# Scores and row maxima trade their banks: a two-layer attention and expert kernel on one core

## The reference

```
xn = layernorm(x)
s  = attention_part(xn)
g  = silu(expert_part(xn))
x  = x + s * g
```

```
scores = einsum('bhsd,bhtd->bhst', q_embed, k_embed) / D ** 0.5
attn   = softmax(scores, axis=-1)
out    = einsum('bhst,bhtd->bhsd', attn, v) @ wo.T
```

## Time and profile before

| | before |
|---|---|
| median of 3 runs | 1664.55 us (1663.07 to 1669.39) |
| the profiled execution | 1678.29 us, span 1676.5 us |
| PE busy | 1125.7 us (67%) |
| DVE busy | 1108.0 us (66%) |
| ACT busy | 684.1 us (41%) |
| POOL busy | 509.7 us (30%) |
| mean granted TensorE clock | 0.778 |

### The profile page before, as it was taken

How to read it: one execution, slowest core, us unless ns; L and a number is a source line. 1 busy time by engine, 2 the same in 40 slices (tenths; PEclk the granted TensorE clock), 3 DMA queues, 4 the chain that set the end, 5 groups by cost and what they waited for, 6 DMA issues and landing times.

```text
span 1676.5 us, 16891 instructions
## 1 busy us (share of the span) xinstructions
PE 1125.7 (67%) x5366; PEld 589.4 (35%) x5366; DVE 1108.0 (66%) x1815; ACT 684.1 (41%) x1166; POOL 509.7 (30%) x513
## 2 busy tenths in 40 slices
PE   4465667677766722446656177999977878787886
PEld 4332334343433410222212023888822322222222
DVE  4388798889998423757775056666666766677761
ACT  1023134434554402213352055344346565666563
POOL 2338843234343141344315604000033030303110
PEclk9987787889988955556576576999977877788785
DMA  8301221222122215130303125555442433333300
GB/s 274 126 19 66 75 81 45 72 77 85 44 93 67 73 37 67 25 62 25 52 14 61 47 38 127 185 191 197 153 76 34 63 49 48 45 52 51 58 22 6
DMA packets 73866, 125.08 MB, mean 75 GB/s; under 512 B 13553, under 2 KB 31154, under 8 KB 73778
## 3 DMA queue, kind: packets, MB, share of 16 engines
q1 hardware_dynamic: 65586, 107.22, 26.4%
q0 software_dynamic: 8192, 16.79, 3.9%
HBM read 57.81 MB, written 40.37 MB: 59 GB/s over the span
## 4 chain that ended last, share of the span: by engine, by line
PE 40%; DVE 21%; issue 12%; ACT 9%; POOL 5%; another core or an unknown queue 4%; DMA 2%; SPq 2%; DVEq 0%; ACTq 0%; POOLq 0%
PE PS L782 7%; PE PS L825 6%; PE PS L802 5%; PE PS L683 4%; ACT P L892 4%; PE PS L844 4%; PE PS L762 3%; DVE MX L1598 3%; PE PS L748 2%; PE PS L635 2%; DVE G L1370 2%; DVE UL L1429 2%; POOL XS0D L1152 2%; DMA KS<-MAG 2%
## 5 line engine op out<-in xcount | busy, mean ns | idle before, releaser
L1598 DVE TENSOR_REDUCE MX<-PS 128x1 f32<-128x512 f32 x512 | 324.2, 684 | 189.9 <-PE PS L762 125.5
L892 ACT ACTIVATE P<-PS 128x512 f32<-128x512 f32 x512 | 278.8, 596 | 274.0 <-PE PS L802 180.6
L802 PE MATMUL PS<-QS,KS 50*128 50x512 f32 x512 | 145.9, 566 | 173.0 <-ACT P L892 133.1
L762 PE MATMUL PS<-KS,QS 48*128 48x512 f32 x512 | 154.8, 602 | 58.0 <-DVE MX L1598 31.8
L782 PE MATMUL PS<-P,V 128*32 128x512 f32 x1024 | 190.2, 826 | 0.0
L1181 POOL DMA_INDIRECT A<-Y1D,POS x64 | 73.6, 1149 | 279.1 <-DMA Y1D<-YE 182.0
L802 PEld LDWEIGHTS PS<-QS,KS 50*128 50x128 f32 x512 | 63.3, 243 | 238.9 <-ACT P L892 178.1
L762 PEld LDWEIGHTS PS<-KS,QS 48*128 48x128 f32 x512 | 60.5, 234 | 219.8 <-issue 97.2
L635 PE MATMUL PS<-G,HEADSUM 128*128 128x400 f32 (+2 forms) x160 | 82.9, 647 | 72.8 <-DVE G L1370 48.8
L683 PE MATMUL PS<-XST,WB 128*128 128x512 f32 x184 | 105.9, 711 | 19.4 <-issue 19.4
L1203 POOL TENSOR_TENSOR MAG<-MAG,EH 128x1024 f32<-128x1024 f32 x8 | 18.8, 2353 | 312.1 <-ACT MAG L892 312.1
(11 more groups left out here) (211 smaller groups left out, 2085.9 us busy)
## 6 DMA issues: line engine op xcount, KB each, us to landing
WH<-W1SD SPq DMA_DIRECT2D x23, 704.0 KB, 4.6
QS<-EH SPq DMA_DIRECT2D x64, 128.0 KB
KS<-EH SPq DMA_DIRECT2D x64, 128.0 KB
WB<-in_wb SPq DMA_DIRECT2D x23, 322.0 KB, 2.8
XS<-XS0D SPq DMA_DIRECT2D x23, 256.0 KB, 3.5
Y0D<-YE SPq DMA_DIRECT2D x23, 256.0 KB, 2.0
XS<-XS1D SPq DMA_DIRECT2D x23, 256.0 KB, 3.8
Y1D<-YE SPq DMA_DIRECT2D x23, 256.0 KB, 2.7
```

Source lines behind the costliest of these rows:

```text
L762: signal(pe.matmul(PS[:, s % 4, :], QS[rows, u % 3, hp, 128 * t:128 * t + 128], KS[rows, u % 3, hp, :], start=True, stop=True), "ms")
L802: signal(pe.matmul(PS[:, 4 + s % 2, :], KS[rows, u % 3, hp, 128 * k:128 * k + 128], QS[rows, u % 3, hp, :], start=True, stop=True), "st")
L892: act.activation(*a, **k).then_inc(sem[name], 1)
L1598: go("mx", dve.tensor_reduce(MX[:, u % 2, t, 4 * par + hp:4 * par + hp + 1], PS[:, s % 4, :], AX.X, ALU.max))
```

## The change

The two kinds of product change their banks. Before, row maxima go in turn through banks 0 to 3 and scores through banks 4 and 5. After, scores go through banks 0 to 3 and row maxima through 4 and 5. One DVE instruction then takes the maxima of both banks of a frame, and one ACT instruction the exponentials of both banks of a frame, so that `mx` and `ex` count pairs. Around the expert block the waits follow the banks: the first row maximum behind it now waits for the last block output to be read (`y1ev`), which before was the wait of the first scores; the first hidden product waits for exponentials, the first block output for maxima.

```
-                if s >= 4 and par == 0:
-                    pe.wait_ge(sem["mx"], s - 2)
+                if s >= 2 and par == 0:
+                    pe.wait_ge(sem["mx"], s // 2)
+                if (u, i) == tuple(AFTER["max"]):
+                    pe.wait_ge(sem["y1ev"], NBLK)
                 rows = slice(64 * par, 64 * par + SROWS)
-                signal(pe.matmul(PS[:, s % 4, :], QS[rows, u % 3, hp, 128 * t:128 * t + 128], KS[rows, u % 3, hp, :],
+                signal(pe.matmul(PS[:, 4 + s % 2, :], QS[rows, u % 3, hp, 128 * t:128 * t + 128], KS[rows, u % 3, hp, :],
                                  start=True, stop=True), "ms")
...
-                pe.wait_ge(sem["ex"], 4 * m + 4)
+                pe.wait_ge(sem["ex"], 2 * m + 2)
...
-                if (u, i) == tuple(AFTER["scores"]):
-                    pe.wait_ge(sem["y1ev"], NBLK)
                 for a in range(2 * half, 2 * half + 2):
                     s = 4 * m + a
-                    if s >= 2 and a % 2 == 0:
-                        pe.wait_ge(sem["ex"], s)
+                    if s >= 4 and a % 2 == 0:
+                        pe.wait_ge(sem["ex"], s // 2 - 1)
...
-                    signal(pe.matmul(PS[:, 4 + s % 2, :], KS[rows, u % 3, hp, 128 * k:128 * k + 128], QS[rows, u % 3, hp, :],
+                    signal(pe.matmul(PS[:, a, :], KS[rows, u % 3, hp, 128 * k:128 * k + 128], QS[rows, u % 3, hp, :],
                                      start=True, stop=True), "st")
...
-                for a in range(2 * half, 2 * half + 2):
-                    s = 4 * m + a
-                    act.wait_ge(sem["st"], s + 1)
-                    if m >= 2:
-                        act.wait_ge(sem["pv"], m - 1)
-                    go("ex", P[:, m % 2, a, :], PS[:, 4 + s % 2, :], ACT.Exp, scale=HD1 ** -0.5)
+                act.wait_ge(sem["st"], 4 * m + 2 * half + 2)
+                if m >= 2:
+                    act.wait_ge(sem["pv"], m - 1)
+                go("ex", P[:, m % 2, 2 * half:2 * half + 2, :], PS[:, 2 * half:2 * half + 2, :], ACT.Exp, scale=HD1 ** -0.5)
...
-                    dve.wait_ge(sem["ms"], s + 1)
                     if i == 0 and u >= 2:
                         dve.wait_ge(sem["one_full"], SHARED["turn", u - 2] + 1)
-                    go("mx", dve.tensor_reduce(MX[:, u % 2, t, 4 * par + hp:4 * par + hp + 1], PS[:, s % 4, :], AX.X,
-                                               ALU.max))
+                    if par:
+                        dve.wait_ge(sem["ms"], s + 1)
+                        go("mx", dve.tensor_reduce(MX[:, u % 2, t].rearrange("p (o h) -> p o h", o=2)[:, :, hp],
+                                                   PS[:, 4:6, :], AX.X, ALU.max))
```

More of the change, by code:

```diff
@@ L766, in turn @@
                 out, full = bank("turn", u)
-                pe.wait_ge(sem["mx"], STEPS * (u + 1))
+                pe.wait_ge(sem["mx"], STEPS // 2 * (u + 1))
                 for t in range(NT):
@@ L816, in hidden @@
                     if q < 2:
-                        pe.wait_ge(sem["mx"], BEFORE["max"])
+                        pe.wait_ge(sem["ex"], BEFORE["scores"])
                     else:
@@ L837, in down1 @@
                 if q == 0:
-                    pe.wait_ge(sem["ex"], 2 * BEFORE["scores"])
+                    pe.wait_ge(sem["mx"], BEFORE["max"] // 2)
                 if c == 0:
```

## The result

Before and after were timed in turn on the same chip, four times each. The kernel before has a median of 1663.81 us (1657.93 to 1669.39), the changed one 1683.16 us (1678.27 to 1688.0): ratio 1.0117, 95% interval 1.0071 to 1.0162. The change costs 19 us. I had forecast 36 us slower, with 1672 to 1738 as the range: the sign and the range hold, the size was about half.

A forecast was written before the change was run, and what follows sets the result against it. The prediction took no single engine as the bound but a loop in which PE and ACT take turns over two score banks. Terms 36 + 5 + 7 + 3 + 1 - 16 gave +36 us, 1664.55 to 1700 us, range 1672 to 1738.

The forecast's parts named there:

- What binds, and the new loop: Regular full-clock frames: the PE and ACT loop of 1.67 us gives way to a PE and DVE loop of 1.94.
- The handoff: Regular full-clock frames: DVE starts 0.66 us after the products, so 0.27 us more for each of 54 frames, 14.6 us.
- The half clock: Main stretch at half clock: two frames take 5.4 against 4.99 us, 0.4 for each of 24 couples, 9.6 us.
- The frames with other DVE work: Main stretch: extra PE to DVE handoffs cost 8 us at `mag` and `hilo`, 4 us at `sum1` and `mix1`.
- The main stretch: From 1212 to 1616.8 us of the profile, with 164 of the 276 frames: 36 us slower.
- The first parts: Ahead of the block: first 20 frames +3 us, then +7 and +5; first maxima behind the block +1.
- The last 20 frames: From 1616.8 to 1660 us, scores without maxima: double banks are pure gain, minus 16 us, between minus 10 and minus 22.
- Merging: One instruction for two banks: maximum 1217 ns, saving 0.07 us a frame; exponential 1.03 against 1.09 us, saving 0.06.
- The clock: Rival, regular frames: the clock falls, the 54 frames take 2.7 instead of 1.94 us, +40, 1740 us; chance 0.15.
- ACT's loop was the dearer one everywhere: Rival, main stretch: PE's 45 us of waits for exponentials in irregular frames go, about 1643 us, faster; chance 0.09.
- The stall under POOL's DMAs: Rival, 892.5 to 962 us: ACT's stall goes by instructions, half as many save 30 us, 1670 us; chance 0.11.

The follow-up runs named there:

- Experiments 1: Kernel before with its banks kept, but one maximum and one exponential instruction for each two banks: ratio 0.9966 to the kernel before.
- 2: Kernel before with the changed kernel's swapped banks but single instructions for each bank, PE waiting for both maxima of the last frame: ratio 1.0169 to the kernel before.
- 7: Changed kernel with maxima over 256 of each bank's 512 columns and exponentials of a tenth of the argument: ratio 0.9821 to the kernel before.
- 8: Kernel before with maxima over 256 of each bank's 512 columns and exponentials of a tenth of the argument: ratio 0.9903 to the kernel before.
- experiments 5: Kernel before, unchanged, profiled again on the same chip as the changed kernel: span 1598.6 us.
- 6: Changed kernel, unchanged, profiled again on the same chip as the kernel before: span 1621.6 us, ratio 1.0139 to the kernel before.
- experiment 3: Kernel before, but the last 20 frames put their scores through banks 0 to 3 in turn: 1575.37 against 1594.02 us, ratio 0.9887.
- experiments 10: Swapped banks with single instructions, PE waiting for each maxima bank by itself: ratio 1.0162 to the kernel before.
- 11: Kernel before with maxima in banks 0 and 1 alone and scores still in 4 and 5: ratio 1.0229 to the kernel before.
- experiment 4: Three pairs of banks 0 to 5 in rotation for maxima and scores alike, with merged instructions: 1577.07 against 1594.02 us, ratio 0.9863 to the kernel before.

## Why the prediction was right in sign and too large in size

**What binds, and the new loop.** Right. The loop of PE and DVE takes the place of that of PE and ACT, on the same frames, and is longer. Experiments 1 and 2 put the loss on the banks alone, 7 and 8 show the maximum inside the loop.

**The handoff, mis-sized.** The step "the pair takes 0.51, so DVE, which now needs both, starts at 0.66" failed: it starts at 0.57 (1619.43 to 1620.00). I had 0.15 us behind the end of a single matmul of 0.386 and set it behind the end of the pair at 0.51; but DVE sees the second product only 0.03 us after the first (0.54). The loop is 1.85 and not 1.94, a couple of regular frames 3.70 for 3.35. The term as a whole came out near its size all the same, by luck: in experiments 5 and 6 the 29 couples of maxima that take 3.2 to 3.5 us before lose 15.4 us (I had 27 couples and 14.6 us). 24 of them lose 9.4 us, 0.39 each. The other five (from frames 94, 138, 156, 220 and 252) lose 6.1 us: there the changed kernel happened to be at half clock for a part of each couple, with single score products of 0.63 us, where the kernel before was at full clock (0.40 to 0.49).

**The half clock, the term with the wrong working.** "0.4 for each of 24 couples, 9.6 us". DVE starts 0.86 us after the products (976.26 to 977.12) and not 0.99, and the frame with `pv` takes 3.01 for my 3.1, so a couple of 5.15 us for 4.99 costs 0.16 us and not 0.4. The number of couples is one execution's too: counted by the exponentials' starts, as I had counted, the first trace of before has 24 couples of 4.75 to 5.15 us and that of experiment 5 has 15. By this working the term would have been 2 to 4 us. The frames at half clock lose more all the same: 9.9 us in the 19 steps that are at half clock in both traces of experiments 5 and 6. They are not couples of 4.99. Seven of the 19 steps are 1.20 us before and 2.13 or 2.14 after, and five are 2.47 to 2.71 before and 3.01 or 3.02 after: at half clock too DVE found frames ready, and a pair of 3.68 us (frames 132 and 133) takes 5.15. The term had no such pair in it. That 9.9 lies near my 9.6 is luck.

**The frames with other DVE work.** I had 8 us at `mag` and `hilo`, and 4 at `sum1` and `mix1` in five places (there are six). Over the six steps that begin at each of the four runs of three maxima ahead of `mag`, the changed kernel loses 2.3 us in all; over the five steps around each `sum1` and `mix1` place, 5.1. The second figure is loose: with the five steps taken one frame later it would be some 9. DVE's timeline at `mag`, before (5):

```profile
1207.67 3.73 DVE L1598 TENSOR_REDUCE MX<-PS 128x1 f32<-128x512 f32 x6
1212.63 2.52 DVE L1528 TENSOR_TENSOR MAG<-MAG,EH 128x1024 f32<-128x1024 f32 x1 [1.23 <-ACT MAG L892]
```

and after (6):

```profile
1224.46 1.23 DVE L1597 TENSOR_REDUCE MX<-PS 128x2 f32<-128x1024 f32 x1
1226.31 1.23 DVE L1597 TENSOR_REDUCE MX<-PS 128x2 f32<-128x1024 f32 x1 [0.62 <-PE PS L764]
1228.17 1.23 DVE L1597 TENSOR_REDUCE MX<-PS 128x2 f32<-128x1024 f32 x1 [0.63 <-PE PS L764]
1229.31 2.55 DVE L1526 TENSOR_TENSOR MAG<-MAG,EH 128x1024 f32<-128x1024 f32 x1
```

The run of 3.73 is drawn out to 4.94, but DVE had then waited 1.23 us for the softplus, and that wait is gone: from the first maximum to `mag` it is 4.96 us before and 4.85 after. The handoffs ahead of `mag` cost nothing net, as the low end of my range had allowed. The main stretch lost 26.3 us for my 36: 2.3 at `mag` and `hilo`, 5.1 at `sum1` and `mix1`, and 18.9 in all other frames, at full and half clock together, where I had 24.2.

**The first parts.** First 20 frames +3.6 for my +3; border +0.85 for +1. From the first score to the block I had +12 and measured +5.8 (3.2 in the first pair); it was priced by the same half-clock couples and `mag` places.

**The last 20 frames.** 14.6 and 14.4 us gained in the two pairs of traces for my 16, and experiment 3 shows that it comes from four banks there, whatever the maxima use. My lower end of 21 us supposed full clock throughout; the clock was 0.81 to 0.88.

**Merging.** 1225 ns for my 1217 and 1025 for 1.03, and a ratio of 0.9966. The cycle counts of the Trainium skill (VectorE: DVE Perf Modes, "The TRN2 errata") give an estimate of 1.19 us for the merged maximum and of 0.125 us saved by each instruction less; the trace has 1.225, and DVE's work fell by 324.2 - 313.6 = 10.6 us for 256 instructions, 0.04 each. By that rule merging would be worth more; the measurement decides, and the earlier trace rows already showed neighbouring instructions overlapping.

**The rivals.** The clock did not fall in the main stretch of the changed kernel: 0.80 and 0.82 before, 0.82 and 0.83 after, and the regular frames run at full clock in rows as those of 1619 to 1627 us. Between the first score and the POOL stream it did fall, from 0.64 to 0.57 in the first pair of traces (and 0.66 to 0.55 in experiments 5 and 6), where that stretch of 150 us became 6 to 7 us longer. The Trainium skill (TensorE: Matmul & The Clock Gate, "A second HAM failure mode: psum-queue depth-cycling") names short idle pieces between groups of matmuls as such a cause; this stretch would agree, the main one doesn't, and no run here separated it from what DVE's routing work does to PE there. In experiments 10 and 11, with two maxima banks as well, the clock of every execution is at or below the lowest of the kernel before (0.788 to 0.796 against 0.796 to 0.809, and 0.764 to 0.776 against 0.777 to 0.801), so this rival had more to it than the changed kernel alone shows. That ACT's loop was the dearer one everywhere is refuted for this change: its score banks give next to nothing beside two maxima banks at equal clock (experiment 11). What they would give beside four maxima banks no run shows; with three pairs in rotation, experiment 4, it is at most 8 us. The stall under POOL's DMAs does not go by instructions: in the changed kernel, with half as many, ACT is held for 53.7 us where it was 73.6, DVE ahead of its maxima for 41.2 where it was 34.7,

```profile
ACT P L892 <- remote: 53.7, 6, 32.6
DVE MX L1597 <- remote: 41.2, 4, 31.0
```

in fewer but longer pieces than in the earlier trace rows, and the stretch is 67.0 us for 69.5.

**The size, in sum.** Of the 36 us, 5.3 went in the main stretch's frames without other DVE work, at full and half clock together, 5.7 with `mag` and `hilo`, 6.2 with the stretches ahead of the block; 1.1 at `sum1` and `mix1`, 0.5 at the start and the border and 1.6 in the last frames came back. That leaves 22 us, and the two timings gave 19 and 22. The mechanism was right; the handoff of each frame, the half-clock couples and the handoffs ahead of `mag` were set too dear, and the frames that DVE found ready at half clock were left out.

## What to carry to other kernels

Count for each pair of engines the loop "filled, read, free again" with the buffers that it has, and give the double buffer to the longer one; here 0.57 + 1.23 + 0.05 us against 1.67. A queue that runs ahead in some frames (steps of 1.20 us among 2.14) is worth its buffers even where its mean load is far from full, and loses it at once with them. Where one kind of work ends earlier, let the other have its buffers from there on: it was the only part of this change that clearly paid, and it paid without the rest. Before two traces are compared, sort their frames by the granted clock in both: experiments 2 and 10 take the same time and differ in both the loop and the clock.

## What the runs showed that I had not expected

Chips differ by more than any edit here. The kernel before took 1594 to 1598 us on three chips and 1664 to 1668 where the first and the last set ran. Most of it lies in one place: while POOL issues 52 indirect DMAs in a row (some 65 us), ACT and DVE stand for up to 32.6 us for something that the trace calls remote in the profiles of the slower sets, also in that of experiment 11:

```profile
DVE MX L1598 <- remote: 42.2, 7, 25.9
```

In the traces of the other sets no such wait appears, and in that of experiment 6 DVE goes on with a maximum each 1.85 us through much of the same stream. First score to block is 303.0 us in the first profile of before and 245.1 in that of experiment 5, 58 of the 78 us by which the spans of these two executions differ; 18 more are in the main stretch. What holds the engines there was not found out.

The clock makes executions of one code differ: from the first to the last maximum behind the block it took 402.6, 384.5 and 373.3 us at clocks of 0.80, 0.82 and 0.85. Between the last two, the 104 steps that are at full clock in both differ by 0.1 us in all, and the 27 at half clock in both by 0.4. A comparison of two traces needs more than one of each, or medians beside it.

Two 48-row products issued one after the other into two banks are both there for DVE 0.57 us after the first starts at full clock, where the first bank alone takes 0.54.
